# Three stages in one program per engine, with each stage's first steps inside the last steps of the one ahead

## The chip, the cores and the metric

The kernel runs on one core of one Trainium2 chip. The metric is the device time of one execution in microseconds (us), lower is better. The time before is 2320.34 us, the median of three runs (2317.63 to 2322.99).

## The reference

The input is `x`, 16 batches of 512 tokens with 256 features, all float32. Four sublayers follow one another, each with a residual sum and a layer norm:

```python
x = layernorm(x + attention(x))      # 16 heads, causal, rotary; keys and queries go through a latent of 32
x = layernorm(x + fp4_ffn(x))        # gate and up 256 -> 704, silu(gate) * up, down 704 -> 256;
                                     # inputs and weights rounded to FP4 in blocks of 16 along the features
x = layernorm(x + recurrence(x))     # state_t = tanh(state_{t-1} @ tanh(a) + x_t @ b), 16 heads of 64 states,
                                     # out_t = state_t @ c + skip * x_t, then x_t + out_t @ w_out + b_out
x = layernorm(x + channel_mix(x))    # needs the token before each token
```

Attention takes one batch at a time and needs all of its tokens. The feed-forward layer takes any token by itself. The recurrence takes one time step of all 16 batches, and each step needs the one before it.

## The kernel before, in words

`program` calls four functions: `attention`, `fp4_ffn`, `recurrence`, `channel_mix`. Each opens a block of its own (`with nc.Block()`), with one program for each of SyncE (SP, which issues the DMAs), GpSimd (POOL), ScalarE (ACT), VectorE (DVE) and TensorE (PE). At the end of a block all engines wait for one another, and SP waits until the block's last store has landed. Between the functions the activations lie in device memory as rows [512 tokens, 16 batches, 256].

**Attention** is written out in full (`straight`). Step i is one batch and has four cycles g = 0 to 3, one for each group of four heads. The work on a group is spread over several cycles, so after the last group (cycle 63) PE still has the product with the values, the transposes, and the two halves of the output projection to do (L717, L645, L733, L573). Then DVE adds the residual and takes the statistics (L430, L480), POOL makes the scale (L302 to L308), ACT writes the normalised rows (L381) and SP stores them (L247). A batch's rows are stored some six cycles after its last group.

**The feed-forward stage** (`fp4_ffn`) has 64 tiles of 128 rows. A tile is 8 time steps of all 16 batches, so the first tile needs all of attention. `pipelined` writes out the steps -4 to 7, loops over 8 steps at a time, and writes out the last 8 steps and 6 more. In step i PE does gate(i) (L1273), the transposes of hidden tile i-2 (L1297), up(i) (L1273), the transposes of input tile i+1 (L1308), and down(i-2) (L1280). DVE does the residual and statistics of tile i-3, the block scales of input tile i+3, one rounding for input tile i+2 and hidden tile i-1 together (L1240 to L1248), and silu times up for tile i (L1255). POOL multiplies by the scales (L1158 to L1170). PE and DVE hand tiles to one another through counts of semaphores. A table of ACT has to be loaded once for the silu.

**The recurrence** has 64 tiles too, of 8 time steps and 16 batches. In each time step PE multiplies the states of two sides q = 0, 1 by the weights (L1570, L1573) and ACT takes the tanh (L1474) of each side, while PE works on the other. Between the time steps of tile i PE puts the other work: mix (L1619, L1622) and project (L1601) of tile i-1, turn (L1647) and the input products `feed` (L1588, L1591) of tile i+1. Ahead of tile 0 lie a block of set-up (clearing the state on DVE, L1480, and the tanh of the weights on ACT, L1460), the normalisation of tile 0, and 58 matmuls that compute nothing of use (`fill`, L1610). The tiles are then in a loop of two tiles a round:

```python
step(-1, 1)
with pe.Fori(0, 2) as again:
    with pe.Fori(again, 1 + (TILES // 2 - 1) * again) as k:
        for j in range(2):
            step(k * 2 + j, j)
    fill(1, TURN, 32, False)
step(TILES, 0)
```

So tiles 0 and 1 run, then 32 `fill` matmuls, then tiles 2 to 63 by the same code, then 32 `fill` again and what is left of tile 63.

**Channel mix** is a block of its own in both kernels.

Of the kernel before, what the change touches and what calls it, by code (L numbers as in the profile page):

```python
# [6 lines left out]
F32 = mybir.dt.float32  # L7
# [6 lines left out]
P = 128  # L14
# [4 lines left out]
FFN = 704  # L19
# [24 lines left out]

def head_of(g, t):

    return 8 * (g // 2) + 2 * t + g % 2
# [13 lines left out]
class FfnWeights:  # L61

    def __init__(self, nc, ctx):
        def sb(name, shape):
            return ctx.enter_context(nc.sbuf_tensor("kept_" + name, shape, F32))

        self.ident = sb("ident", [P, P])
        self.w_upT = sb("w_upT", [P, CC, 2 * FFN])
        self.w_downT = sb("w_downT", [P, DOWN_CHUNKS, DIM])  # L70
        self.loaded = ctx.enter_context(nc.semaphore("kept_loaded"))

def attention(nc, a, x1_dram, kept):

    with ExitStack() as ctx:
        def sb(name, shape, dt=F32):
            return ctx.enter_context(nc.sbuf_tensor(name, shape, dt))

        def sem(name):  # L80
            return ctx.enter_context(nc.semaphore(name))

        ps_near = ctx.enter_context(nc.psum_tensor("ps_near", [P, GROUP, SEQ], F32))
        near = [ps_near[:, t, :] for t in range(GROUP)]
        far = [ctx.enter_context(nc.psum_tensor(f"ps_far{t}", [P, SEQ], F32))[:] for t in range(GROUP)]

        squares = sb("squares", [P, 2, P])
        ident, blocks = squares[:, 0, :], squares[:, 1, :]
        mask = sb("mask", [P, SEQ])
        ident_bf = sb("ident_bf", [P, P], BF16)  # L90
        ones_bf = sb("ones_bf", [P, P], BF16)
        cos_sin = sb("cos_sin", [P, 2, SEQ])
        cos_t, sin_t = cos_sin[:, 0, :], cos_sin[:, 1, :]
        columns = sb("columns", [P, 10])
        b_attn = columns[:, 0:6]
        q2l_b, kv2l_b, l2o_b, wqk_b = (columns[:, 6 + n:7 + n] for n in range(4))
        probsT = sb("probsT", [P, 2, GROUP, TURNED])
        w_v = probsT[:, 1, GROUP - 1, TURNED - CC * DIM:].rearrange("p (s c) -> p s c", c=DIM)
# [4 lines left out]
        kv2l_rep, l2o_rep = reps[:, 0, :], reps[:, 1, :]  # L103
        bd_v = sb("bd_v", [P, P])
        wc_t = sb("wc_t", [P, CC, DIM])
        cv = sb("cv", [P, CC, DIM])
        by = sb("by", [P, CC])
        by_all = sb("by_all", [P, CC, P])
        bias_row = sb("bias_row", [P, DIM])
        exponent = sb("exponent", [P, QT])  # L110
        eps = sb("eps", [P, QT])

        xT = sb("xT", [P, CC, SEQ])
        xtok = sb("xtok", [P, QT, DIM])
        xb = sb("xb", [P, QT, DIM])
# [6 lines left out]
        k_swap = sb("k_swap", [P, 2, SEQ])  # L122
        Q = sb("Q", [P, GROUPS, SEQ])
        K = sb("K", [P, GROUPS, SEQ])
        V = sb("V", [P, 2, QT, HEADS, LATENT])
# [16 lines left out]

        quantiser = WeightQuantiser(nc, ctx, kept, ident, sem)
# [64 lines left out]

        FIRST_LOADS, LOADS = 16 * 5, 16 * 6

        with nc.Block() as block:
            @block.sync
            def _(sp):
                FIRST = ((w_qk16, a["c_attn_wT"].rearrange("(c p) n -> p c n", p=P)), (columns, a["columns"]), (w_lat, a["w_lat"]),
                         (cos_sin, a["cos_sin"]), (w_qf, a["w_qf"]))
                THEN = ((reps, a["reps"]), (squares, a["squares"]), (w_v, a["c_attn_w_v"].rearrange("(s p) c -> p s c", p=P)),
                        (wc_t, a["cproj_wT"].rearrange("(s p) c -> p s c", p=P)), (bias_row, a["cproj_b"].partition_broadcast(P)),
                        (mask, a["mask"]))
                sp.dma_start(xT[:], a["xT"][0, :, :].rearrange("(c p) t -> p c t", p=P)).then_inc(xT_loaded, 16)
                for dst, src in FIRST:  # L220
                    sp.dma_start(dst[:], src).then_inc(first_loaded, 16)
                for dst, src in THEN:
                    sp.dma_start(dst[:], src).then_inc(loaded, 16)

                def swap(b, g):

                    sp.wait_ge(k_sin_ready, cyc(1, b, g, 3))
                    for i in range(2):
                        sp.dma_start(k_swap[i:P:2, g % 2, :], k_sin[1 - i:P:2, g % 2, :]).then_inc(k_swapped[g % 2], 16)

                def swap_latent(b, g):

                    s = (g + 1) % 2
                    sp.wait_ge(q_turned, cyc(2, b, g, 7))
                    for i in range(2):
                        sp.dma_start(q_swap[i:P:2, s, :], q_sin[1 - i:P:2, s, :]).then_inc(q_swapped[s], 16)

                def step(i, j, k):
                    if isinstance(i, int) and i == -1:
                        sp.dma_start(kept.ident[:], a["ident"]).then_inc(kept.loaded, 16)  # L240
                    for g in range(GROUPS):
                        if g == 1 and exists(i, 0):
                            await_count(sp, xb_ready, i)
                            sp.dma_start(xtok[:], a["x"][bass.ds(i, 1), :, :].rearrange("a (t p) c -> p (a t) c", p=P)).then_inc(xtok_loaded, 16)
                        if g == 2 and exists(i, -2):
                            sp.wait_ge(x1_ready, i - 1)
                            sp.dma_start(x1_dram[:, bass.ds(i - 2, 1), :].rearrange("(t p) a c -> p t (a c)", p=P), x1[:]).then_inc(x1_stored, 16)  # L247
                        if g == 3 and exists(i, 2):
                            sp.wait_ge(V_full, 2 * i + 4)
                            sp.dma_start(xT[:], a["xT"][bass.ds(i + 2, 1), :, :].rearrange("a (c p) t -> p (a c) t", p=P)).then_inc(xT_loaded, 16)  # L250
                        if runs(i, g, 3):
                            swap_latent(i, g)
                        if runs(i, g, 2):
                            swap(i, g)
                        if is_cycle(i, g, 0):
                            quantiser.load(sp, a)
                pipelined(sp, step, BATCH, 2, 1, 2)
                sp.wait_ge(x1_stored, 16 * BATCH)

            @block.gpsimd  # L260
            def _(pool):
                nc.gpsimd.memset(shift[:], 0.0)
                nc.gpsimd.memset(ones_bf[:], 1.0)
                nc.gpsimd.memset(V[:, :, :, :, HEAD_DIM:HEAD_DIM + 1], 1.0)
                nc.gpsimd.memset(V[:, :, :, :, HEAD_DIM + 1:], 0.0)
                nc.gpsimd.memset(eps[:], LN_EPS)
                nc.gpsimd.memset(exponent[:], -0.5)
                nc.gpsimd.memset(zero[:], 0.0).then_inc(constants, 1)
                pool.wait_ge(constants, 1)
                pool.wait_ge(first_loaded, FIRST_LOADS)  # L270

                def add_latent(b, g):

# [6 lines left out]
                def turn_keys(b, g):  # L280
# [5 lines left out]
                    if runs(b, g, 3):  # L286
                        add_latent(b, g)
# [1686 lines left out]
```

## Time and profile before

| what | us |
|---|---|
| median of 3 runs | 2320.34 |
| the profiled execution: its time | 2320.48 |
| its span | 2318.7 |
| attention, by the trace | 0 to 1031.6 |
| feed-forward | 1031.6 to 1577.9 |
| recurrence | 1577.9 to 2114.0 |
| channel mix | 2114.0 to 2318.7 |

How to read it: the stages follow one another without overlap, so the time is their sum. Inside a stage the timeline of an engine gives start, length, line and, in square brackets, the idle time ahead of an instruction and what ended it.
### The profile page before, as it was taken

What the parts mean: (1) busy time and instruction counts of PE and PEld (TensorE: products, weight loads), DVE (VectorE), ACT (ScalarE), POOL (GpSimd) and SP (SyncE); (2) the same over time, 40 slices, a digit from 0 to 9 for tenths busy, and PEclk for the clock granted to TensorE, in tenths of its full rate; (3) what the DMA queues carried; (4) which work ended last, traced back from release to release, by engine and by line L of the source; (5) the groups of instructions that cost most, each with busy time, mean ns of one, the idle gap of its engine ahead of it and who ended that gap; (6) DMA issues with size and microseconds to landing.
All of it is one profiled execution on the core that took longest, in us unless ns stands there. A gap on an engine that the chain in (4) does not pass through costs nothing. (4 is left out here: it accounts for less than half of the span.)

```text
span 2318.7 us, 90879 instructions
## 1 busy us (share of the span) xinstructions
PE 2209.4 (95%) x36556; PEld 1542.3 (67%) x36556; DVE 1706.9 (74%) x4854; ACT 1060.6 (46%) x2707; POOL 1187.8 (51%) x1674
## 2 busy tenths in 40 slices
PE   6999999999999999959999999997999999997997
PEld 3556665556655555536777777776888888885775
DVE  3788888888887777749999999982555555454997
ACT  2656565655666665532222222231444444442444
POOL 3555555655555555525666666662444444441333
PEclk8999999999999999989999999997999999998999
DMA  2211111111111111120100000100101011011232
GB/s 92 91 56 64 57 65 65 65 63 58 57 64 65 65 61 60 52 69 22 33 32 32 32 32 32 34 20 29 32 32 36 32 34 33 32 32 46 84 95 77
DMA packets 101627, 117.73 MB, mean 51 GB/s; under 512 B 10672, under 2 KB 80080, under 8 KB 101456
## 3 DMA queue, kind: packets, MB, share of 16 engines
q1 hardware_dynamic: 101456, 115.44, 15.1%
q8 instruction: 108, 1.77, 0.3%
q14 instruction: 63, 0.52, 0.1%
HBM read 48.29 MB, written 33.55 MB: 35 GB/s over the span
## 5 line engine op out<-in xcount | busy, mean ns | idle before, releaser
L1474 ACT ACTIVATE r_state<-ps_state 128x64 f32<-128x64 f32 x1024 | 228.6, 223 | 295.8 <-PE ps_state L1573 290.7
L1570 PE MATMUL ps_state<-r_state,later_pairs_a 64*64 64x32 f32 x8192 | 334.4, 219 | 19.4 <-ACT r_state L1474 12.5
L1570 PEld LDWEIGHTS ps_state<-r_state,later_pairs_a 64*64 64x64 f32 x8192 | 295.2, 135 | 79.2 <-issue 60.7
L1573 PE MATMUL ps_state<-r_state,later_pairs_a 64*64 64x32 f32 x8192 | 334.6, 220 | 2.8 <-issue 2.8
L423 DVE CUSTOM_DVE_ANT_0 ps_near<-ps_near,mask 128x512 f32<-128x512 f32 (+1 forms) x512 | 270.5, 589 | 89.5 <-PE ps_near L519 89.3
L295 POOL TENSOR_SCALAR_AFFINE_SELECT probsT<-probsT 128x512 f32<-128x512 f32 x256 | 159.8, 636 | 271.2 <-ACT probsT L406 168.0
L1573 PEld LDWEIGHTS ps_state<-r_state,later_pairs_a 64*64 64x64 f32 x8192 | 288.8, 135 | 3.1 <-issue 3.1
L423 DVE CUSTOM_DVE_ANT_0 ps_far<-ps_far,mask 128x384 f32<-128x384 f32 (+1 forms) x512 | 198.3, 457 | 32.7 <-PE ps_far L519 31.7
L1158 POOL TENSOR_TENSOR f_fp<-f_rounded,f_scale 128x960 f32<-128x960 f32 (+2 forms) x67 | 117.3, 1750 | 166.2 <-DVE f_rounded L1248 166.2
L527 PE MATMUL ps_far<-Q,K 32*128 32x256 f32 (+2 forms) x1536 | 180.9, 415 | 1.2 <-ACT probsT L403 0.5
L1181 ACT ACTIVATE f_silu<-ps_gate 128x704 f32<-128x704 f32 x64 | 48.5, 758 | 288.5 <-PE ps_gate L1273 288.5
L1280 PE MATMUL ps_down<-kept_w_downT,f_hT 128*128 128x256 f32 x768 | 176.6, 380 | 1.9 <-ACT f_hT L1186 1.9
L519 PE MATMUL ps_near<-K,Q 32*128 32x512 f32 (+1 forms) x1024 | 165.5, 527 | 9.4 <-POOL K L290 6.3
L406 ACT ACTIVATE probsT<-ps_far 128x512 f32<-128x512 f32 x256 | 132.2, 603 | 89.8 <-PE ps_far L533 89.8
L1273 PE MATMUL ps_gate<-kept_w_upT,f_xT 128*128 128x352 f32 x512 | 164.2, 464 | 1.4 <-ACT f_xT L1195 1.4
L527 PEld LDWEIGHTS ps_far<-Q,K 32*128 32x128 f32 x1536 | 129.1, 183 | 49.9 <-issue 24.9
L1273 PE MATMUL ps_up<-kept_w_upT,f_xT 128*128 128x352 f32 x512 | 162.1, 459 | 0.0
L1452 POOL TENSOR_TENSOR r_veps<-r_mv,r_eps 128x1 f32<-128x1 f32 x64 | 12.2, 190 | 283.8 <-DVE r_mv L1537 283.8
L717 PE MATMUL ps_near<-probsT,V 128*32 128x512 f32 (+3 forms) x2048 | 152.8, 439 | 3.6 <-POOL probsT L295 2.8
L1280 PEld LDWEIGHTS ps_down<-kept_w_downT,f_hT 128*128 128x128 f32 x768 | 141.0, 190 | 19.1 <-ACT f_hT L1186 2.4
L284 POOL TENSOR_TENSOR k_sin<-K,cos_sin 128x512 f32<-128x512 f32 x64 | 81.2, 1269 | 129.1 <-ACT K L367 129.1
L423 DVE DVE_READ_ACCUMULATOR2_ANT top<- 128x1 f32 x1024 | 142.8, 139 | 0.0
(213 smaller groups left out, 5401.1 us busy)
## 6 DMA issues: line engine op xcount, KB each, us to landing
q_swap<-q_sin SPq DMA_DIRECT2D x128, 128.0 KB, 2.1
k_swap<-k_sin SPq DMA_DIRECT2D x128, 128.0 KB, 2.1
xT<-in_xT_dram SPq DMA_DIRECT2D x16, 512.0 KB, 3.6
xtok<-in_x_dram SPq DMA_DIRECT2D x16, 512.0 KB, 3.8
x_rows<-x SPq DMA_DIRECT2D x16, 512.0 KB, 2.9
f_x<-x_rows SPq DMA_DIRECT2D x64, 128.0 KB, 2.0
x_rows<-f_x SPq DMA_DIRECT2D x64, 128.0 KB, 1.7
r_x<-x_rows SPq DMA_DIRECT2D x64, 128.0 KB, 2.1
```

The lines of the kernel that those rows point to most:

```text
L295: return nc.gpsimd.affine_select(block, block, pattern=[[0, GROUP], [1, P]], compare_op=ALU.is_ge, fill=0.0, base=0, channel_multiplier=-1)
L406: nc.scalar.activation(mine[:, t, AT[1]:AT[1] + SEQ], far[t], ACT.Exp).then_inc(exped, 1)
L423: nc.vector.tensor_tensor_reduce(bank[:, at:at + width], bank[:, at:at + width], mask[:, SEQ - width:SEQ], 1.0, -3e38, ALU.add, ALU.max, t ...
L519: out = nc.tensor.matmul(bank[:, at:at + width], Q[rows, g, qi * P:(qi + 1) * P], K[rows, g, 0:width], start=True, stop=True, skip_group_c ...
L527: return nc.tensor.matmul(bank[:, at:at + SEQ - kj * P], K[rows, g, kj * P:(kj + 1) * P], Q[rows, g, kj * P:SEQ], start=(kj != 3), stop=Fa ...
L717: out = nc.tensor.matmul(near[0][LATENT * t:LATENT * (t + 1), kj * P:SEQ], V[:, jp, kj, head_of(gp, t), :], probsT[:, gp % 2, t, AT[kj]:AT ...
L1158: nc.gpsimd.tensor_tensor(blocks(parts(fp4[:, s, :], i, BLOCK)), blocks(parts(rounded[:, s, :], i, BLOCK)), spread(parts(scale[:, s, :], i ...
L1273: out = nc.tensor.matmul(ps[:, half, 0:HALF], xT[:, j % 2, c, :], w_upT[:, c, at + half * HALF:at + (half + 1) * HALF], start=(c == 0), st ...
L1280: out = nc.tensor.matmul(ps_down[:, 0:DIM], hT[:, j % 2, kd, :], w_downT[:, kd, :], start=(kd == 0), stop=(kd == KD - 1))
L1474: nc.scalar.activation(state[:, j % 2, banks, :, t, 0, :], sums[:, j % 2, banks, :, now], ACT.Tanh).then_inc(state_ready[t], 1)
L1570: nc.tensor.matmul(sums[half(v), j % 2, stays, c, now], A[half(v), 3 * q, c, :], last[half(v), stays, c, :], start=False, stop=True, skip_ ...
L1573: out = nc.tensor.matmul(sums[half(1 - v), j % 2, changes, c, now], A[half(v), 3 * q + 1 + was, c, :], last[half(v), changes, c, :], start ...
```

## The change

Attention, the feed-forward stage and the recurrence now share one block. Each of them returns its five engine programs (`Programs`) in place of running them, and for the feed-forward stage each is an object `Steps`, whose `to(n)` issues the steps up to n. The attention programs call `feed.to` inside their last cycles, and the recurrence programs call it ahead of and inside their first tile.

```diff
+class Steps:
+    def to(self, end):
+        unroll = self.unroll
+        while self.at < end:
+            if self.at == unroll and end >= self.tiles - unroll > unroll:
+                with self.engine.Fori(1, self.tiles // unroll - 1) as k:
+                    for j in range(unroll):
+                        self.step(k * unroll + j, j, k)
+                self.at = self.tiles - unroll
+            else:
+                self.step(self.at, self.at % unroll, self.at // unroll)
+                self.at += 1
```

Where attention calls it (cycle 63 is the last group, 64 to 67 the four after it; here and for the recurrence below, the added lines are put together by engine):

```diff
 # SP
+if is_cycle(i, g, CYCLES - 2):
+    sp.wait_ge(quantiser.copied, len(quantiser.fills))
+    feed.to(4)
 # POOL, around the first affine select of the last group, and after cycle 65
+if is_cycle(i, g, CYCLES - 1): feed.to(-2)
+if is_cycle(i, g, CYCLES - 1): feed.to(0)
+if is_cycle(i, g, CYCLES + 1): feed.to(3)
 # ACT: after yT of cycle 63; after its last Exp; after cycle 65
+if is_cycle(i, g, CYCLES - 1): feed.to(0)
+if is_cycle(i, g, CYCLES - 1): feed.to(1)
+if is_cycle(i, g, CYCLES + 1): feed.to(3)
 # DVE: after y of cycle 63; then behind the attention work of cycles 64, 65 and 67
+if is_cycle(i, g, CYCLES - 1): feed.to(0)
+if is_cycle(i, g, CYCLES): feed.to(1)
+elif is_cycle(i, g, CYCLES + 1): feed.to(2)
+elif is_cycle(i, g, CYCLES + 3): feed.to(3)
 # PE: ahead of the product with the values of the last group; and behind cycles 63, 65 and 67
+if is_cycle(i, g, CYCLES):
+    pe.wait_ge(exped, 12 * CYCLES - 2)
+    feed.to(1)
...
+if is_cycle(i, g, CYCLES - 1):
+    pe.wait_ge(exped, cyc(12, i, g, 4))
+    feed.to(0)
+elif is_cycle(i, g, CYCLES + 1):
+    feed.to(2)
+elif is_cycle(i, g, CYCLES + 3):
+    pe.wait_ge(z_added, 2 * BATCH)
+    feed.to(3)
```

A feed-forward tile is now 128 tokens of one batch, in rows 16 KB apart; tile n of the first 16 waits only for batch n's store, and the loads of the recurrence's weights move from step 0 to step 12 (`LATER`). SP's part is written out for all 64 tiles:

```diff
+def rows(dram, n):
+    return dram[n // BATCH * P:(n // BATCH + 1) * P, n % BATCH, :]
...
+if n < BATCH:
+    sp.wait_ge(x1_stored, 16 * (n + 1))
+sp.dma_start(x[:, n % UNROLL, :], rows(x1_dram, n)).then_inc(x_loaded[n % UNROLL], 16)
```

The second half of the last output projection goes to another PSUM bank (`near[2]`), so it no longer waits for DVE to empty the first. The PSUM banks of the stages and the SBUF tiles are laid out so that the first steps use what the stage ahead has left.

At the recurrence (FED is 64, LAST_FED is 2; feed-forward step 64 is the hidden transposes and down of tile 62, step 65 those of tile 63):

```diff
 # SP
+feed.to(FED - 8); wait for the first 16 stores; steps.to(1); feed.finish(); steps.finish()
 # POOL: the clearing of the state between feed-forward steps 4 to 7
+feed.to(FED - 2); steps.to(-1); feed.to(FED - 1); steps.to(0); feed.finish(); steps.finish()
 # ACT
+feed.to(FED); nc.scalar.activation(A[:], A[:], ACT.Tanh); feed.to(FED + 1)
+# and feed.to(FED + 2) at time step LAST_FED of tile 0
 # DVE
+measure(-2, 2, -1); feed.to(FED - 1); normalise(-2, 2); measure(-1, 3, -1)
+feed.to(FED); normalise(-1, 3); turned(-1, 3); feed.finish(); steps.finish()
 # PE
+feed.to(FED)
+pe.wait_ge(xn_ready, 1); turn(-1, 1, MIX[1])
+feed.to(FED + 1)
+pe.wait_ge(xT_ready, 1); pe.wait_ge(*fed[0])
+for c in range(CC): out = inputs(-1, c)
...
+step(0, 0)                       # with feed.finish() ahead of time step LAST_FED
+with pe.Fori(0, 2) as again:
+    with pe.Fori(again, 1 + (TILES // 2 - 2) * again) as k:
+        for j in (1, 2):
+            step(k * 2 + j, j % 2)
+    fill(0, TURN, 32, False)
+step(TILES - 1, 1)
 step(TILES, 0)
```

Tile 0 and tile 63 are now written out ahead of and behind PE's loop, with tiles 1 and 2 in its first round. The 58 `fill` matmuls ahead of tile 0 are gone; those behind the first round and behind the loop stay, the latter now ahead of tile 63. Tile 0 leaves out mix and project, tile 63 leaves out turn and `feed`. `feed(j, c)` of before is called `inputs(j, c)`.

## Rows read from the trace of the kernel before

**Rows 1.** The profile page: each engine's busy time, its share and instructions.
```profile
PE 2209.4 (95%) x36556; PEld 1542.3 (67%) x36556; DVE 1706.9 (74%) x4854; ACT 1060.6 (46%) x2707; POOL 1187.8 (51%) x1674
```
**Rows 2.** Windows: start:end, length, busy time of each engine, PEclk, DMA.
```profile
1003.00:1031.60 28.60, 12.43 (x136) 6.78 (x136) 7.51 (x24) 7.64 (x17) 7.16 (x12) 0.84 0.11 37
1031.60:1061.89 30.29, 21.55 (x75) 13.94 (x76) 24.28 (x57) 5.89 (x10) 9.56 (x14) 0.81 0.31 98
1061.89:1553.99 492.10, 492.10 (x2162) 366.00 (x2161) 464.20 (x957) 142.07 (x299) 332.21 (x420) 1.00 0.10 31
...
1588.18:1601.20 13.02, 9.80 (x358) 8.17 (x360) 1.39 (x5) 3.57 (x16) 3.98 (x9) 0.80 0.08 23
1601.20:1614.50 13.30, 12.61 (x346) 10.78 (x341) 3.96 (x12) 3.57 (x16) 1.93 (x7) 0.50 0.01 4
1614.50:1620.70 6.20, 6.20 (x44) 4.35 (x33) 0.00 (x0) 0.00 (x0) 1.38 (x2) 0.57 0.15 45
1620.70:1628.40 7.70, 7.47 (x348) 6.31 (x346) 3.68 (x12) 3.57 (x16) 0.90 (x3) 1.00 0.00 0
```
**Rows 3.** Timeline of PE at the end of attention: start, us, line, count, idle.
```profile
1008.73 4.06 PE L717 MATMUL ps_near<-probsT,V 128*32 128x512 f32 x32 [2.81 <-POOL probsT L295]
...
1017.06 1.93 PE L573 MATMUL ps_near<-wc_t,yfT 128*32 128x256 f32 x32 [1.01 <-DVE yfT L490]
...
1019.91 1.93 PE L573 MATMUL ps_near<-wc_t,yfT 128*32 128x256 f32 x32 [0.91 <-DVE z L430]
...
1037.94 0.66 PE L1308 MATMUL ps_xT<-kept_ident,f_fp 128*128 128x128 f32 x2 [16.10 <-POOL f_fp L1158]
```
**Rows 4.** Timeline of DVE and of ACT behind the last projection.
```profile
1021.91 0.69 DVE L430 TENSOR_TENSOR z<-ps_near,xb 128x512 f32<-128x512 f32 x1 [2.06 <-PE ps_near L573]
...
1022.64 1.41 DVE L480 BATCH_NORM_STATS2 stats<-z 128x6 f32<-128x256 f32 x4
...
1026.20 2.07 ACT L381 ACTIVATE x<-z,centre,rstd 128x256 f32<-128x256 f32 x4 [10.79 <-POOL centre L308]
```
**Rows 5.** Timeline of PE: the parts of step 3 of the feed-forward stage.
```profile
1061.89 2.53 PE L1273 MATMUL ps_gate<-kept_w_upT,f_xT 128*128 128x352 f32 x8
1064.25 0.82 PE L1297 MATMUL ps_hT<-kept_ident,f_fp 128*128 128x128 f32 x6
1064.91 2.53 PE L1273 MATMUL ps_up<-kept_w_upT,f_xT 128*128 128x352 f32 x8
...
1067.50 2.75 PE L1280 MATMUL ps_down<-kept_w_downT,f_hT 128*128 128x256 f32 x12
```
**Rows 6.** DMA issues of the page: attention's stores, KB each, us to landing.
```profile
x_rows<-x SPq DMA_DIRECT2D x16, 512.0 KB, 2.9
```
**Rows 7.** Timeline of PE: from the last feed-forward tiles to the recurrence.
```profile
1561.97 0.82 PE L1297 MATMUL ps_hT<-kept_ident,f_fp 128*128 128x128 f32 x6
...
1563.72 2.86 PE L1280 MATMUL ps_down<-kept_w_downT,f_hT 128*128 128x256 f32 x12 [0.94 <-ACT f_hT L1186]
...
1578.85 6.21 PE L1610 MATMUL ps_state<-r_quiet 128*128 128x256 bf16 x40 [6.09 <-ACT later_pairs_a L1460]
...
1595.48 0.30 PE L1573 MATMUL ps_state<-r_state,later_pairs_a 64*64 64x32 f32 x3 [2.13 <-issue]
...
1600.49 0.49 PE L1588 MATMUL ps_state<-r_xT,later_pairs_b 32*64 32x64 f32 x7 [0.94 <-issue]
```
**Rows 8.** DMA traffic within 1593 to 1594 us: the instruction queue, one fetch.
```profile
q8 instruction: 1, 0.02, 5.7%
```
**Rows 9.** Timeline of DVE: the same instruction of tiles 3 and 5.
```profile
1632.35 0.61 DVE L1517 TENSOR_SCALAR r_xT<-ps_state,later_recurrence_columns 128x128 f32<-128x128 f32 x2 [1.46 <-PE ps_state L1647]
...
1647.91 0.61 DVE L1517 TENSOR_SCALAR r_xT<-ps_state,later_recurrence_columns 128x128 f32<-128x128 f32 x2 [1.46 <-PE ps_state L1647]
```
**Rows 10.** Timeline of PE in and behind the recurrence's last tile.
```profile
2101.81 0.29 PE L1591 MATMUL ps_state<-r_xT,later_pairs_b 32*64 32x128 f32 x1 [0.52 <-DVEq L1542]
...
2103.23 3.67 PE L1610 MATMUL ps_state<-r_quiet 128*128 128x256 bf16 x32
```

More of the change, by code:

```diff
@@ L1 @@
+from collections import namedtuple
 from contextlib import ExitStack
@@ L819, in attention_arrays @@
+            straight(step)
+        return Programs(sync, gpsimd, scalar, vector, tensor), early, x1_stored, (exped, 12 * CYCLES)
 def attention_arrays(inputs):
@@ L1323, with recurrence @@
 STEPS = P // BATCH
-def recurrence(nc, ident, weights, x2_dram, x3_dram):
+def recurrence(nc, sems, memory, banks, ident, weights, x2_dram, x2_stored, fed, x3_dram):
     TILES = TOKENS // P
@@ new lines, in recurrence, with exists, later, half @@
+    x3_stored = [sem(f"x3_stored{s}") for s in range(2)]
+    def exists(i, d):
+        return not isinstance(i, int) or 0 <= i + d < TILES
+    def later(i, d, n):
+        return not isinstance(i, int) or i + d >= n
+    def half(v):
+        return slice(v * STATE, (v + 1) * STATE)
+    def steps_of(t, parity):
+        return t.rearrange("p (n e b) -> p n e b", e=2, b=BATCH)[:, :, parity, :]
+    LEAD, LAG = 3, 4
+    FED = TILES
+    LAST_FED = 2
+    def sync(sp, feed):
+        def step(i, j, k):
+            if exists(i, 3):
+                if later(i, 3, UNROLL):
+                    sp.wait_ge(twice_ready, i + (4 - UNROLL))
+                sp.dma_start(x[:, (j + 3) % UNROLL, :], x2_dram[bass.ds((i + 3) * P, P), :]).then_inc(x_loaded[(j + 3) % UNROLL], 16)
+            if exists(i, -3):
+                sp.wait_ge(x3_ready, i - 2)
+                sp.dma_start(x3_dram[bass.ds((i - 3) * P, P), :], x3[:, (j + 1) % 2, :]).then_inc(x3_stored[(j + 1) % 2], 16)
+        steps = Steps(sp, step, TILES, UNROLL, LEAD, LAG)
+        feed.to(FED - 8)
+        for stored in x2_stored:
+            sp.wait_ge(stored, 16 * (BATCH // 2))
+        steps.to(1)
+        feed.finish()
+        steps.finish()
+        for stored in x3_stored:
+            sp.wait_ge(stored, 16 * (TILES // 2))
@@ new lines, in scalar, with step @@
+    def scalar(act, feed):
+        feed.to(FED)
+        act.wait_ge(weights.loaded, 16 * weights.LOADS)
+        nc.scalar.activation(A[:], A[:], ACT.Tanh).then_inc(w_tanh, 1)
+        feed.to(FED + 1)
+        def step(i, j, k):
+            for t in range(STEPS):
+                if isinstance(i, int) and i == 0 and t == LAST_FED:
+                    feed.to(FED + 2)
+                if exists(i, 0):
+                    for q in range(SIDES):
+                        if t == 0:
+                            act.wait_ge(inputs_in, i + 1)
+                        act.wait_ge(summed[q], i * STEPS + (t + 1))
+                        if t == 0 and later(i, 0, 2):
+                            act.wait_ge(mix_full, 2 * i)
+                        now, banks = slice(t * BATCH, (t + 1) * BATCH), slice(2 * q, 2 * q + 2)
+                        nc.scalar.activation(state[:, j % 2, banks, :, t, 0, :], sums[j % 2][:, banks, :, now], ACT.Tanh).then_inc(state_ready[t], 1)
+        steps = Steps(act, step, TILES, UNROLL, LEAD, LAG)
+        steps.to(1)
+        feed.finish()
+        steps.finish()
```

2151 lines of the change are left out of this document (1094 added, 1057 removed).

## The prediction

> **What bounds the kernel now.** I read the page's busy times first. PE is busy for 2209.4 of 2318.7 us [rows 1], so a change that removes no PE work can win only in the gaps, or where PE is busy but slow. The view of windows then says where these are [rows 2]. From 1061.89 to 1553.99 PE is busy all the time: 60 feed-forward tiles, 492.10 / 60 = 8.20 us each. Its order there is gate, transposes, up, transposes, down [rows 5]. DVE is busy for 464.20 / 60 = 7.74 us a tile, close behind. From tile 3 on the recurrence repeats every (1647.91 - 1632.35) / 2 = 7.78 us a tile [rows 9]. Neither rate is touched. Three stretches are bad. (a) From 1003 to 1061.89 PE has 12.43 + 21.55 us of work in 58.9 us [rows 2]: the tail of attention, a barrier, and a pipeline that fills. PE idles 16.10 us in one piece ahead of the first feed-forward transposes [rows 3]. (b) From 1561.97, the hidden transposes of tile 62, to the first recurrence matmul at 1588.18: 26.2 us with two tiles' down in it. (c) From 1588.18 to 1628.40 the recurrence does three tiles in 40.2 us where 3 x 7.78 = 23.3 would do. The reader should see PEclk fall to 0.50 there and stay for all of tile 1 [rows 2].
>
> The sum is made against the profiled execution: 2320.48 us, of which the span is 2318.7. The median of the runs, 2320.34, is the same to 0.14 us. All times below are on the clock of the trace of before.
>
> **Change (a), attention to feed-forward.** I replay the order written in the diff until PE starts the gate of tile 3, which was at 1061.89 and from which PE never waits. A step of feed-forward on PE has the parts gate 2.36, hidden transposes 0.66, up with input transposes 2.59, down 2.6 (starts apart) [rows 5].
> - Steps -4 to -1 need DVE and POOL, which have little to do in cycle 63. I cost them at nothing, covered by PE's and ACT's work on the last group, but for 0.9 us on PE and ACT (two transposes, a copy, and the scores that wait behind them). If that cover is not there, PE waits for up to 6 us, from DVE's work in the stretch that begins at 1031.60 (24.28 us, of which some 6 lie ahead of the first gate) [rows 2].
> - Step 0 on PE (gate, up, transposes: 5.0 us) goes ahead of the product with the values. PE idled there from 1008.73 - 2.81 = 1005.92 [rows 3]; with the 0.9 it starts at 1006.8 and ends at 1011.8. The product took 4.06 us [rows 3] with PEclk at 0.50 after that idle time; with PE kept busy I take 2.4, down to 1014.2 against 1012.8. So step 0 costs the tail 1.4 us.
> - Copy, transposes, division and transposes again (4.3 us before, 1012.8 to the next projection at 1017.06) shift by 1.4, and step 1, for which the projection now waits, begins at 1017.9 at the latest. It ends at 1022.9. The two halves of the projection, 1.93 each [rows 3], end at 1026.8.
> - DVE is in program order too: it begins step 1 at about 1019, has 7.7 us of it, then adds the two halves, 0.69 each [rows 4]: 1028.1. PE waits for this count before step 2.
> - Step 2 on PE, 8.2 us: gate of tile 3 at 1036.4.
> - Behind DVE's step 2 come the last batch's statistics and POOL's scale (1026.20 - 1022.64 = 3.6 us up to ACT's start) and ACT's write (2.07) [rows 4]: 1028.1 + 0.7 + 7.8 + 3.6 + 2.1 = 1042.3, ahead of ACT's silu and copy of step 3. PE wants that copy for down at 1043.5 and gets it at 1044.9: 1.4 us.
> Gain: 1061.89 - 1036.4 - 1.4 = 24.1 us. Bounds: at most 27 (no stall in step 3, and the product hides step 0); at least 12, if step 3 as a whole waits behind the last batch's rows.
>
> The order of tiles costs nothing that I can find. The loads run four tiles, 33 us, ahead; the trace does not show 1 KB rows at 16 KB distance for 128 KB, but attention's stores of four times as much have that distance and land in 2.9 us [rows 6]. Even 10 us a load would be hidden. SP's loads of tiles 8 and later stand behind the last batch's store, at about 1044, and tile 8 is wanted after 1054.
>
> **Change (b), feed-forward to recurrence.** PE's step 63 ends at 1561.97. Then, in order: the turn of tile 0 (0.4), hidden transposes of tile 62 (0.8), ACT's copy (0.94 idle) [rows 7], down (2.8): 1566.9. DVE's part for tile 0, some 3 us over steps 61 to 63, lies in its slack of 8.20 - 7.74 us a tile and in the shorter last steps. The input products take 0.9 us: time step 0 begins at 1567.8, not at 1588.18. The 58 `fill` (6.21 us for 40 of them) [rows 7], the set-up and the barrier fall away. After two time steps (1.9) tile 63's transposes, copy and down come in, 0.8 + 0.9 + 2.7 = 4.4 us in which the recurrence stands still: 1574.1. Six more time steps at 0.97: tile 0 ends at 1580. At full clock without stalls the old tile 0 would have ended at 1588.18 + 7.78 = 1595.96. This part is worth 16 us. The bound below is 11: DVE a whole 5 us late with tile 0's input.
>
> **(c) The slow start of the recurrence.** In tile 0 PE stands for 2.13 us with nothing to wait for ("issue"), and 0.94 us again at its end [rows 7]. A fetch on the instruction queue falls in the first gap [rows 8]: this is code that runs for the first time, at 348 / 7.70 = 45 matmul records a microsecond when nothing stops it [rows 2]. Then the clock is 0.50; tile 1 takes 13.30 us, and the 32 `fill` take 6.20 us and bring 1.00 back [rows 2]. In the new order all of tile 0 is first-time code, and so are tiles 1 and 2, the loop's first round. The 4.4 us of slow work inside tile 0 let the fetching catch up, so I put the same stall of 2.1 at the end of tile 0 and the fall right behind it. Then tiles 1 and 2 are both at half clock: 1580 + 2.1 + 2 x 13.3 + 6.2 = 1614.9 for the start of tile 3, against 1628.4. So of the 16 us here 13.5 are left. This is the term with ends far apart. If the clock never falls, it is 1580 + 15.6 + 3.7 = 1599.3, a gain of 29; if the stall comes in tile 0's third time step, five steps more at half clock cost 3 and the gain is 10.
>
> **The end.** Tile 63 leaves out turn, `feed` and a wait of 0.52 [rows 10]: 0.4 + 0.9 + 0.5 = 1.8 saved. The `fill` of 3.67 only changes place. But tile 63 is now first-time code: I add the stall of 2.1 and 2.0 for three time steps at half clock, which is what tile 0 paid from 1595.5 to 1601.2 (5.7 against 3.7). Net +2.3, bounds -1.8 and +4.
>
> Here the Trainium skill speaks otherwise ("Runtime: NRT & Kernel Launch", section "Instruction fetch mechanics"): the prefetch is sequential, straight code is mostly hidden by the issue rate, and it is taken branches that stall. By that rule the first run of a straight tile would cost nothing. The row with 2.13 us of "issue" in code that is reached without a backward branch disagrees, so I go by the row; what the rule would make of the time is the first rival.
>
> Two small edits go together: the clearing of the state moves to POOL between early feed-forward steps, under 1 us a piece. POOL is busy for 332.21 of 492.10 us [rows 2] and idles before each of its multiplications, so it is hidden; if not, it costs 2 us once.
>
> **Sum.** -24.1 - 13.5 + 2.3 = -35.3: 2320.48 - 35.3 = 2285 us.
>
> **Rivals.**
> 1. *The clock stays up.* For it: PE comes out of dense work, and the down of tile 63 lies inside tile 0. The rule of the Trainium skill named above ("Runtime: NRT & Kernel Launch", "Instruction fetch mechanics"), that straight code is fetched in time, would have this result. Against it: PE starved at this code rate once [rows 2, 7]. Then -24.1 - 29 - 1.8 = -55: 2265 us.
> 2. *The steps of the two stages get into each other's way at (a).* In-order engines: ACT's write of the last batch or DVE's two sums hold up the filling pipeline. For it: three engines carry both, and DVE has 7.7 us of work a step ahead of each small piece of the tail. Against it: the positions in the replay fit. Then (a) gives 12 to 14: 2295 to 2297 us.
> 3. *Slower: the clock is not regained.* The `fill` after the first round is what brought 1.00 back. If a fall comes behind it, say when PE jumps back to the loop's start, nothing in the recurrence restores it, since tile 1 alone at 13.30 us a tile did not. Each tile then costs 13.3 - 7.8 = 5.5 us, and it decides from the seventh tile (35 / 5.5); over 61 tiles 2285 + 336 = 2621 us. Against it: the same `fill` before the same backward jump held it for 62 tiles.
> 4. *It does less than it says:* a wait that I have not seen serialises one of the seams, (a) or (b), and the time is 2300 to 2318, or no change.
>
> **How the numbers follow.** Forecast 0.55, rival 1 0.14, rival 2 0.18, rival 3 0.04, rival 4 0.09, of which 0.03 is within 0.2% (5 us, about what a measurement of this kernel can tell from no change) and 0.01 slower. The forecast's own range is 2276 to 2291, from the ends of (c) and of the tail. The range 2264 to 2300 takes in rivals 1 and 2 and leaves out 0.13. Faster 0.92, same 0.03, slower 0.05.
>
> **What would show it.** In the changed trace: the gate of tile 3 near 1036 to 1040, PE without a gap over 3 us between 1003 and 1040, and no half clock at the product with the values (a); from the hidden transposes of tile 62 to the first L1570 matmul 6 us, where it was 26.2 (b); a gap named "issue" of about 2 us near the end of tile 0, PEclk 0.50 over the two tiles behind it and 1.00 after the `fill` (c); a second such gap in tile 63. Wrong would be: DVE's sum of the last projection more than 3 us behind it, the gate of tile 3 after 1045, PEclk at 1.00 all the way, or 0.50 behind the first round.

## The result, and the profile after

The changed kernel takes 2283.43 us (median of 4, 2282.18 to 2286.24); the kernel before took 2320.43 beside it (2317.63 to 2322.99). The ratio is 0.984, with a 95% interval of 0.9825 to 0.986. The forecast was 2285, so the sum came out. Its terms did less well: the one for the end of the recurrence was off by 4.1 us, those for (a) and (c) by 1.6 and 1.4 us in the opposite direction, so the closeness of the sum is in part luck. One of the 35 executions of the kernel before, which stands in no ratio here and has no trace, took 3662.56 us at a mean granted clock of 0.543.

The profiled execution took 2283.54 us with a span of 2281.8, which is 36.9 less than the span of before. The page's line for the engines, which answers to [rows 1]:

```profile
PE 2199.1 (96%) x36408; PEld 1534.9 (67%) x36408; DVE 1706.3 (75%) x4852; ACT 1060.1 (46%) x2707; POOL 1191.2 (52%) x1676
```

PE has only 10.3 us less work, so 26.6 of the 36.9 came out of its gaps. The view of windows, as in [rows 2] (start:end, length, busy time of each engine with its instructions, PEclk, DMA share, GB/s), shows the stretches that answer to those of before:

```profile
994.00:996.00 2.00, 0.59 (x4) 0.51 (x8) 1.86 (x8) 1.36 (x3) 1.05 (x2) 0.86 0.00 0
996.00:1002.00 6.00, 5.19 (x32) 1.29 (x28) 3.24 (x12) 2.06 (x4) 2.55 (x5) 0.50 0.00 0
1003.00:1037.92 34.92, 31.55 (x255) 20.41 (x244) 26.75 (x60) 12.10 (x24) 15.93 (x18) 1.00 0.05 16
1047.56:1531.46 483.90, 483.90 (x2126) 359.96 (x2125) 456.89 (x940) 140.22 (x295) 327.89 (x423) 1.00 0.12 36
1545.30:1557.00 11.70, 10.23 (x340) 8.44 (x341) 3.64 (x11) 5.36 (x21) 5.38 (x17) 1.00 0.05 15
1557.00:1562.00 5.00, 3.16 (x138) 2.61 (x133) 0.69 (x2) 1.68 (x8) 2.16 (x4) 1.00 0.19 56
1562.00:1587.00 25.00, 21.17 (x543) 17.29 (x535) 7.23 (x22) 5.56 (x25) 6.62 (x16) 0.50 0.08 24
1587.00:1593.30 6.30, 6.30 (x61) 4.62 (x58) 0.00 (x0) 0.24 (x2) 0.00 (x0) 0.54 0.14 43
1593.30:1601.50 8.20, 8.00 (x359) 6.65 (x357) 3.57 (x11) 3.57 (x16) 0.74 (x2) 1.00 0.00 0
2063.30:2071.00 7.70, 6.93 (x321) 5.93 (x320) 2.54 (x8) 3.57 (x16) 0.74 (x2) 1.00 0.02 5
```

The reader should see five things. The tail of attention now has PE busy for 31.55 of 34.92 us at full clock. The steady feed-forward tile is what it was: 483.90 / 59 = 8.20 us from the gate of tile 4 to that of tile 63. The recurrence's tile 0 runs at full clock (1545.30 to 1557.00). The clock then stands at 0.50 from 1562 until the `fill` brings it back, up to 1593.3. And tile 63 (the last line) is at 1.00 from end to end.

The seam between attention and feed-forward, timeline of PE, answering to [rows 3 to 5]:

```profile
995.41 2.09 PE L580 MATMUL ps_near<-Q,K 32*128 32x512 f32 x8 [1.67 <-ACT shiftT L401]
998.73 4.09 PE L773 MATMUL ps_near<-probsT,V 128*32 128x512 f32 x32 [0.81 <-ACT probsT L415]
...
1009.43 2.63 PE L1342 MATMUL ps_gate<-kept_w_upT,f_xT 128*128 128x352 f32 x8 [0.54 <-ACT probsT L448]
1011.90 2.53 PE L1342 MATMUL ps_up<-kept_w_upT,f_xT 128*128 128x352 f32 x8
...
1014.58 2.36 PE L773 MATMUL ps_near<-probsT,V 128*32 128x512 f32 x32
...
1029.61 2.63 PE L1342 MATMUL ps_gate<-kept_w_upT,f_xT 128*128 128x352 f32 x8 [0.86 <-DVE z L475]
...
1037.92 2.53 PE L1342 MATMUL ps_gate<-kept_w_upT,f_xT 128*128 128x352 f32 x8
...
1044.86 2.86 PE L1349 MATMUL ps_down<-kept_w_downT,f_hT 128*128 128x256 f32 x12 [1.18 <-ACT f_hT L1259]
1047.56 2.53 PE L1342 MATMUL ps_gate<-kept_w_upT,f_xT 128*128 128x352 f32 x8
```

Gate 0 stands ahead of the last product with the values, which takes 2.36 us where it took 4.06; gate 3 is at 1037.92. The last gap before the steady tiles is the 1.18 us for ACT's copy in step 3.

The seam between feed-forward and recurrence, answering to [rows 7]: PE, and then ACT's tanh, of which there is one per time step.

```profile
1539.65 0.82 PE L1368 MATMUL ps_hT<-kept_ident,f_fp 128*128 128x128 f32 x6
1541.41 2.86 PE L1349 MATMUL ps_down<-kept_w_downT,f_hT 128*128 128x256 f32 x12 [0.94 <-ACT f_hT L1259]
...
1548.51 2.86 PE L1349 MATMUL ps_down<-kept_w_downT,f_hT 128*128 128x256 f32 x12 [0.94 <-ACT f_hT L1259]
1561.03 0.24 PE L1687 MATMUL ps_state<-r_state,later_pairs_a 64*64 64x32 f32 x1 [1.78 <-issue]
```
```profile
1545.82 0.46 ACT L1575 ACTIVATE r_state<-ps_state 128x64 f32<-128x64 f32 x2 [3.96 <-PE ps_state L1690]
1546.60 0.46 ACT L1575 ACTIVATE r_state<-ps_state 128x64 f32<-128x64 f32 x2 [0.32 <-PE ps_state L1690]
1551.80 0.46 ACT L1575 ACTIVATE r_state<-ps_state 128x64 f32<-128x64 f32 x2 [2.84 <-PE ps_state L1690]
...
1558.37 0.46 ACT L1575 ACTIVATE r_state<-ps_state 128x64 f32<-128x64 f32 x2 [0.58 <-PE ps_state L1690]
1561.38 0.48 ACT L1575 ACTIVATE r_state<-ps_state 128x64 f32<-128x64 f32 x2 [2.56 <-PE ps_state L1690]
```

From the hidden transposes of tile 62 to the first recurrence matmul it is 5.6 us, where it was 26.2. The jump from 1546.60 to 1551.80 is tile 63's down inside tile 0 (a normal step is 0.8 to 1.0, so 4.4 are added). The jump to 1561.38 is the first stall: two time steps of tile 1 are done, and PE stands still in the third for "issue". Three more such gaps follow, the last of them longer than the first:

```profile
1566.79 0.21 PE L1687 MATMUL ps_state<-r_state,later_pairs_a 64*64 64x32 f32 x1 [0.97 <-issue]
...
1571.78 0.32 PE L1687 MATMUL ps_state<-r_state,later_pairs_a 64*64 64x32 f32 x2 [0.98 <-issue]
...
1584.66 0.21 PE L1687 MATMUL ps_state<-r_state,later_pairs_a 64*64 64x32 f32 x1 [1.88 <-issue]
```

Where the 36.9 us came from, in differences between the same two events of each trace:

| stretch | before | after | gain |
|---|---|---|---|
| attention's start to the gate of tile 63 | 1553.99 | 1531.46 | 22.5 |
| gate of tile 63 to the first tanh | 34.7 | 14.4 | 20.4 |
| first tanh to tile 3's first tanh | 40.2 | 48.5 | -8.3 |
| tile 3's first tanh to channel mix | 485.1 | 483.3 | 1.8 |
| channel mix | 204.6 | 204.1 | 0.5 |

### The profile page after: what moved, and what is told of

Read it like the earlier page. It is cut to its first block and busy times, and to the rows that moved or that the text cites. A ratio compares the mean times of both kernels' runs of the same rounds, so it can differ in the third digit from the quotient of the medians.

```text
span 2281.8 us, 90273 instructions
## 1 busy us (share of the span) xinstructions
PE 2199.1 (96%) x36408; PEld 1534.9 (67%) x36408; DVE 1706.3 (75%) x4852; ACT 1060.1 (46%) x2707; POOL 1191.2 (52%) x1676
```

## The experiments

Each was timed beside the kernel before on its chip. "Start" below is the time from the gate of tile 63 to tile 3's first tanh in the run's trace: 62.9 us in the changed kernel, 75.0 before. It leaves out what moves ahead of the seam.

**e1: no feed-forward steps inside attention.**

```diff
-if is_cycle(i, g, CYCLES - 1): feed.to(...)     # all calls of POOL, ACT, DVE and PE in attention
-...
 if is_cycle(i, g, CYCLES + 3):
     pe.wait_ge(z_added, 2 * BATCH)
-    feed.to(3)
```

> The changed kernel without the feed-forward steps inside attention: GpSimd, ScalarE, VectorE and TensorE begin step -4 only when their own attention work is done; one block, per-batch tiles and early loads stay. Theory (the steps inside the tail hide the filling of the pipeline; the barrier is the smaller part): VectorE can start filling at about 1024.5 us instead of 1033.6, so the gate of tile 3 comes near 1053 (1061.9 before, 1037.9 changed); time about 2298 us, 14 to 16 above the changed kernel. Rival (dropping the barrier and the store-and-load round trip is what pays, the interleaving adds little): 2284 to 2287 us.

2298.61 us (2298.43 to 2303.34), ratio 0.991 (0.989 to 0.993). PE's timeline shows what is left of the seam:

```profile
1011.92 2.36 PE L750 MATMUL ps_near<-probsT,V 128*32 128x512 f32 x32 [2.81 <-POOL probsT L330]
...
1029.55 0.66 PE L1353 MATMUL ps_xT<-kept_ident,f_fp 128*128 128x128 f32 x2 [7.33 <-POOL f_fp L1203]
1030.67 4.28 PE L1313 MATMUL ps_gate<-kept_w_upT,f_xT 128*128 128x352 f32 x8 [0.46 <-ACT f_xT L1239]
```

So the steps inside attention are worth 15 of the 22.5 us. The other 7 come from what this kernel still has: one block in place of three, the early loads and the order of the tiles.

**e2: e1, and the tiles in the old order.** SP's early loads go too, since the first of them now waits for the last store.

```diff
 # SP, in attention
-feed.to(4)
...
-return dram[n // BATCH * P:(n // BATCH + 1) * P, n % BATCH, :]
+return dram.rearrange("t b c -> (t b) c")[n * P:(n + 1) * P, :]
...
-if n < BATCH:
-    sp.wait_ge(x1_stored, 16 * (n + 1))
+if n == 0:
+    sp.wait_ge(x1_stored, 16 * BATCH)
```

> As the kernel without steps inside attention, and the feed-forward tiles are again 128 consecutive rows (8 time steps of all batches), so the first load waits for the last batch's store. Theory (tiles of one batch cost nothing in the steady state and are worth only the wait for the last store): first load at about 1031 us, gate of tile 3 near 1061, time about 2305 us, 7 to 9 above the kernel without heads; steady feed-forward tile 8.20 us in both. Rival (rows 16 KB apart slow the stage): steady tile below 8.20 us here, and the time at or under that of the kernel without heads.

2309.73 us (2306.71 to 2312.83), ratio 0.9955 (0.994 to 0.997), 11.1 more than e1. The first gate is at 1040.18 against 1030.67: 9.5 of it.

```profile
1039.06 0.66 PE L1352 MATMUL ps_xT<-kept_ident,f_fp 128*128 128x128 f32 x2 [15.65 <-POOL f_fp L1202]
1040.18 5.06 PE L1312 MATMUL ps_gate<-kept_w_upT,f_xT 128*128 128x352 f32 x8 [0.46 <-ACT f_xT L1238]
```

The wait is the 16.10 of [rows 3] again. A tile of one batch pays by itself, before any step is moved, because it needs one batch's store only. One block without the barrier brings next to nothing at this seam: from DVE's last sum of attention (1023.48 here, 1021.91 before) to the gate of tile 3 it is 40.1 us, where it was 40.0. Nor do rows 16 KB apart cost anything: from the gate of tile 4 to that of tile 63 both e1 and e2 take 485.6 us.

**e3: tile 63's down ahead of tile 0.** The pause of 4.4 us is put in front of the first-time code.

```diff
-    LAST_FED = 2
+    LAST_FED = 0
```

> The last feed-forward tile is finished ahead of time step 0 of the recurrence instead of ahead of time step 2. Theory A (a pause in the dense code lets the instruction fetch catch up, and the next stall comes some 8 us of dense work after it): the stall that is in time step 2 of tile 1 comes two time steps earlier, at the border of tiles 0 and 1, and the half clock with it; tile 3 starts 1 to 3 us later against the gate of tile 63, about 0.8 of it because TensorE waits for the last transposes' input; time about 2285.5 us. Theory B (the stall sits at a fixed place in the code): the stall stays in time step 2 of tile 1; only the 0.8 us is lost, 2284.2 us.

2287.69 us (2286.79 to 2290.26), ratio 0.985 (0.984 to 0.987); start 66.2, 3.3 more. The stall (1.51 us of "issue") is again in the third time step of tile 1, as B had it, but the time is 3.5 us over B's. 1.0 of that is a new wait of the hidden transposes for POOL. Another 1.7 is what it brings about: the clock is at 0.50 from 1551.3 to 1554.7 us, and tile 63's down takes 4.54 us in place of 2.86.

**e4: tile 63's down later in tile 0.**

```diff
-    LAST_FED = 2
+    LAST_FED = 5
```

> The last feed-forward tile is finished ahead of time step 5 instead of 2. Theory A (pause lets the fetch catch up): the stall moves three time steps later, to about time step 5 of tile 1, fewer time steps run at half clock: tile 3 starts about 2 us earlier against the gate of tile 63, 2281.4 us. Theory B (fixed place in the code): the stall stays in time step 2 of tile 1 and the time within 0.5 us of the changed kernel's 2283.4.

2283.28 us (2279.25 to 2284.25), ratio 0.983 (0.981 to 0.985); start 60.8. The third time step of tile 1 has no gap now; the first one ends at 1569.29 (2.50 us of "issue"), in the sixth time step.

**e5: a pause of 12 `fill` behind tile 0.**

```diff
         step(0, 0)
+        fill(0, TURN, 12, False)
         with pe.Fori(0, 2) as again:
```

> Edit: 12 more fill matmuls (0.117 us each at full clock, 1.4 us) between recurrence tile 0 and the loop. Theory (the first-time code is fetched more slowly than PE runs through it, and any 1.4 us in which PE needs no new code pushes the stall later): the stall of 1.9 us, now after time step 1 of tile 1, comes some six time steps later or more, so six or more time steps run at full clock instead of half (0.6 to 0.7 us each): +1.4 - 4 to 5 = about 2280 us against 2283.4. Rival (the stall belongs to a fixed place of the code): stall after time step 1 of tile 1 again, +1.4, 2284.8 us.

2281.16 us (2279.32 to 2282.82), ratio 0.983 (0.981 to 0.985); start 60.6, with its 1.4 us in it. The longest gap (2.22 us) is in the sixth time step of tile 1. The rival's fixed place is not gone: a gap of 1.10 us still stands in the third time step, but the clock stays at 1.00 behind it until 1569.5. Three time steps were won, not six.

**e6: a short `fill` ahead of tile 63.** This asks for the term that the prediction had wrong: why tile 63, first-time code too, had no stall.

```diff
-            fill(0, TURN, 32, False)
+            with pe.Fori(0, 4 - 3 * again):
+                fill(0, TURN, 8, False)
```

> Edit: of the 32 fill matmuls ahead of the recurrence's last tile only 8 are left (0.9 us instead of 3.7); those behind the loop's first round stay at 32. Theory A (tile 63, first-time code, ran without a stall because the fill gives the fetch 3.7 us in which PE needs no new code): a stall of some 2 us inside tile 63 and half clock behind it, so the 2.8 us saved are given back: 2283 to 2285 us. Rival B (tile 63 needs no such pause): no stall, the 2.8 us are a gain, 2280.6 us.

2281.48 us (2281.01 to 2283.54), ratio 0.983 (0.982 to 0.985). The median looks like B and the trace like A. From tile 3's first tanh to channel mix it is 482.9 us against 483.3, so of 2.6 us less `fill` 0.4 are left. PE's timeline and the windows at the end of this kernel's recurrence:

```profile
2058.09 1.05 PE L1727 MATMUL ps_state<-r_quiet 128*128 128x256 bf16 x8
...
2066.41 0.23 PE L1690 MATMUL ps_state<-r_state,later_pairs_a 64*64 64x16 f32 x2 [0.65 <-issue]
...
2068.38 1.98 PE L1718 MATMUL ps_state<-later_w_outT,r_outs 64*64 64x256 f32 x16 [0.21 <-DVE r_outs L1636]
```
```profile
2066.00:2068.00 2.00, 1.17 (x52) 1.07 (x52) 0.44 (x2) 0.45 (x2) 0.64 (x2) 0.99 0.00 0
2068.00:2070.00 2.00, 1.79 (x23) 0.80 (x16) 0.58 (x2) 0.00 (x0) 0.00 (x0) 0.50 0.22 74
```

With the pause cut short a stall appears, and half clock behind the last time step. From the first tanh of tile 63 to its last it is 1.26 us more, and from there to channel mix 0.89. The median's 2 us came from the start (61.2), whose code was not edited. There the gap in the third time step of tile 1 was only 0.96 us, and the long one, 2.78 us, stood in the sixth.

**e7: the recurrence's start not interleaved.** Every engine finishes feed-forward first; no barrier and no `fill` come back.

```diff
 # POOL, ACT, DVE and PE, ahead of their part of the recurrence
-feed.to(FED - 2); feed.to(FED)
+feed.finish()
```

> Edit: at the recurrence's start every engine first finishes the feed-forward stage and then begins its part of the recurrence (no barrier, attention's seam unchanged). Theory (the steps of the two stages lying inside each other are worth 12 to 13 us here, of which the barrier and the 58 fill matmuls are a part): 2292 to 2298 us. Rival (the gain came from the fill matmuls and the barrier alone, interleaving is worth nothing): within 3 us of 2283.4.

2294.45 us (2293.86 to 2295.82), ratio 0.989 (0.987 to 0.990), 11.0 above the changed kernel; start 73.5. PE stands idle for 4.12 and 2.50 us for DVE's part, the clock falls ahead of the first time step, and tile 0 is at 0.50 as well.

**e8: a short `fill` behind the first round.** This tries the slower rival's price.

```diff
-            fill(0, TURN, 32, False)
+            with pe.Fori(0, 1 + 3 * again):
+                fill(0, TURN, 8, False)
```

> Edit: of the 32 fill matmuls behind the loop's first round (tiles 1 and 2) only 8 are left; those ahead of tile 63 stay at 32. Theory (the recurrence's own matmuls do not bring the clock back; it is the fill that does): tiles 3 to 62 stay at half clock, 60 x (13.3 - 7.8) = +330 us less 4.5 for the missing fill, about 2609 us. Rival (the recurrence brings its clock back by itself, or 8 fills do): 2279 to 2300 us.

Four executions: 2282.23, 2576.01, 2280.55 and 2573.01 us. The mean granted clock was 0.982 in the first and 0.837 in the second. Neither theory had both. The first is the one with a trace (start 57.9 us, the missing `fill` less).

**e9: one `fill` behind the first round.**

```diff
-            fill(0, TURN, 32, False)
+            with pe.Fori(0, 1 + 31 * again):
+                fill(0, TURN, 1, False)
```

> Edit: behind the loop's first round 1 fill matmul is left of 32; the 32 ahead of tile 63 stay, each with one jump of a loop. With 8 left, two of four executions took 2281 us and two 2575. Theory (the clock stands at half after tile 2 in every execution, the recurrence's own work does not raise it, and dense matmuls behind the first round do; 8 of them reach that point in some executions only): with 1 left every execution is slow, 2574 to 2580 us, PEclk 0.50 from tile 1 to the fill ahead of tile 63. Rival (which executions are slow is chance of another kind, not the length of the fill): fast and slow executions again.

2584.62 us (2583.11 to 2585.39), ratio 1.113 (1.110 to 1.115): all four executions took this long. One window over 37 tiles, and DVE's same instruction in two of them:

```profile
1590.00:2063.00 473.00, 472.72 (x12932) 396.28 (x12928) 149.93 (x448) 133.67 (x599) 122.17 (x296) 0.50 0.06 21
```
```profile
1593.80 0.61 DVE L1609 TENSOR_SCALAR r_xT<-ps_state,later_recurrence_columns 128x128 f32<-128x128 f32 x2 [2.92 <-PE ps_state L1747]
1606.42 0.61 DVE L1609 TENSOR_SCALAR r_xT<-ps_state,later_recurrence_columns 128x128 f32<-128x128 f32 x2 [2.92 <-PE ps_state L1747]
```

PE is busy for 99.9% of 473 us and the clock stays at 0.50. A tile takes 12.62 us instead of 7.78. The recurrence does not bring its clock back by itself; the `fill` does.

**e10: both pauses.** The edits of e4 and e5 in one kernel.

```diff
-    LAST_FED = 2
+    LAST_FED = 5
...
         step(0, 0)
+        fill(0, TURN, 12, False)
```

> Edit: LAST_FED = 5 in place of 2, and 12 fill matmuls between tile 0 and the loop (both fills of 32 stay). Theory (each pause in which PE needs no new code puts off the stall and with it the half clock): the two add up, LAST_FED 5 being worth about 2 us by the trace of the start (tile 3 at 60.8 instead of 62.9 us behind the gate of tile 63) and the fill ahead 2.3 by the medians: 2279 us, tile 1 at full clock throughout. Rival (one pause is enough, a second only costs its own length): 2281 to 2285.

2281.01 us (2280.15 to 2282.45), ratio 0.982 (0.980 to 0.984); start 60.6. The longest gap (2.50 us) ends at 1566.01, in the sixth time step of tile 1, where it is with either pause alone. The two don't add up; the theory of pauses that add is wrong here.

**e11: the changed kernel again**, with no edit, and **e12: e10 and the short `fill` of e6**, timed side by side.

> The changed kernel itself, once more, for two questions that one profile left open. Theory (where the stall in the recurrence's first-time code comes, and whether the clock falls at the last output projection but one, vary from execution to execution of the same code): another time step for the stall, between the tenth and the fifteenth of the recurrence, and the gate of feed-forward tile 63 anywhere within 3 us; median 2283.4 again. Rival (both are fixed by the code, and what e3 to e10 moved they moved by their edits): stall in front of the third time step of tile 1 and PEclk 0.50 at 996 to 1002 us again.

> Edit: LAST_FED = 5, 12 fill matmuls between tile 0 and the loop, and 8 of the 32 ahead of tile 63 left; the one to beat is the changed kernel of the same call. Theory (each is worth what its own run gave: the pauses 2.4 us together, the short last fill 0.5 by its trace): 2280.5 us, 2.9 under the changed kernel. Rival (the differences of 2 us between these medians are chance of the call): within 1 us of the changed kernel.

e11 took 2284.41 us (2280.13 to 2287.38), e12 2280.29 (2277.67 to 2284.20); ratios 0.983 (0.981 to 0.985) and 0.9815 (0.980 to 0.983). e12 is 4.1 us under e11, though the two ranges overlap. The traces give 3.3 of it to the start (60.1 against 63.4) and nothing to the short `fill` (483.7 in both behind it; e12 has gaps of 0.55 and 1.02 us in tile 63, e11 none). e11's first stall was in tile 1's third time step again, its gate of tile 63 at 1534.64 where it had been 1531.46. e12 has the lowest median: 3 to 4 us below the changed kernel's own (2283.4 and 2284.4), and 0.7 below e10's.

## Why the prediction was right, and where it was not

**(a) 24.1 us predicted, 22.5 measured.** The replay held at every step that it named: gate 0 ahead of the product, 2.36 us for the product, 0.86 of waiting for DVE's two sums (predicted 1.3), step 3's stall 1.18 (predicted 1.4). One reason in it is not borne out: that the product takes 2.4 us because PE is kept busy. In e1 and e2 PE idles ahead of it for 2.81 us as before, and it takes 2.36 us too, at a clock of 1.00. e1 and e2 show the two halves: 15.2 us for the moved steps (median of e1 against the changed kernel's) and 10.4 for the tile order (gate of tile 63 at 1546.98 in e1, 1557.37 in e2), less the 3.4 by which e2 is behind the 1553.99 of before (1.6 of that it had lost in attention already, and 1.7 in feed-forward tiles 6 to 9, as e1 did). The replay began from the time of before at 1003 us, and there it lost 2.6 us. At 995 to 1002 the clock was 0.50 behind an idle time of 1.67 us, so scores took 2.09 and the product with the values 4.09 us. In the trace of before, the same idle time at the same place left it at 1.00:

```profile
995.69 1.14 PE L527 MATMUL ps_near<-Q,K 32*128 32x512 f32 x8 [1.67 <-ACT shiftT L361]
997.87 2.36 PE L717 MATMUL ps_near<-probsT,V 128*32 128x512 f32 x32 [0.82 <-ACT probsT L375]
```

It is not the moved steps that do it: e1 has none, and its product took 4.50 us. The windows of e1 to e12 all show 0.50 within 996 to 1004. The trace of before had its half clock one cycle earlier, and for 3.4 us in place of 6.8:

```profile
981.60:985.00 3.40, 3.40 (x19) 2.01 (x21) 0.42 (x1) 0.71 (x2) 0.00 (x0) 0.51 0.00 0
```

What decides between the two was not settled; before has only the one trace.

**(b) 20.4 predicted, 20.4 measured, and the freeze of 4.4 as well.** That "such a seam is a barrier and 58 `fill`" would be the wrong reading. e7 has neither and loses 11.0 us, since PE idles for DVE and the clock falls at once.

**(c) 13.5 predicted, 12.1 measured.** The mechanism held: PE stalls for "issue" in first-time code, and the clock is at half behind it until the `fill`. The prediction had one stall of 2.1 us, at the end of tile 0. The trace has the first two time steps later, in tile 1 (1.78 us), and three more behind it (0.97, 0.98 and 1.88 us), of which the sum had only the 0.68 us that lies in its 13.30 for a tile. The later start wins two time steps at full clock, some 1.3 us, and the further gaps take it back and more. The Trainium skill's rule ("Runtime: NRT & Kernel Launch", "Instruction fetch mechanics"), that straight code is mostly hidden by the issue rate, would have had no stall. The trace of the changed kernel and those of e1 to e12 all have one, the longest gap in each between 1.5 and 2.8 us. The row of the prediction was the better guide.

**The end: +2.3 predicted, -1.8 measured.** This step failed: "tile 63 is now first-time code: I add the stall of 2.1 and 2.0 for three time steps at half clock". Tile 63 is first-time code, but it stands behind 3.7 us of `fill`, in which PE runs 32 matmuls. The prediction said that slow work lets the fetching catch up, used that for tile 0, and did not use it here. e6 shows it: with 8 `fill` a stall comes (0.65 us in one piece), and half clock behind the last time step. e12, with the same 8, has gaps of 0.55 and 1.02 us there. In e6 tile 63 and what follows it up to channel mix cost 2.2 us more, not the 4.1 that was put down; 8 `fill` are a pause too, and without any the case wasn't tried.

The two errors of 1.6 and 1.4 on the gains and this one of 4.1 nearly cancel. With channel mix's unforeseen 0.5 that is 36.9 for 35.3. The 0.5 is not shown to be an effect of the change: the stage takes 203.6 to 204.8 us in the traces of e1 to e12, where its code is the same. That the sum came out is luck to this extent.

**The slower rival** was priced at 5.5 us a tile, from a tile that had stalls of its own in it. e9 measured 12.62 - 7.78 = 4.84, and 301 us in all, where 336 was said. Its mechanism is real and was nearer than a chance of 0.04 sounds: with 8 in place of 32 `fill`, two of four executions took as long as e9's, at the same mean clock (0.837 and 0.838; e9 0.833). They have no trace.

**Where the gaps stand.** The traces answer a question that e3 to e6 and e10 left. The gaps stand at fixed borders in PE's code, some 245 matmuls and weight loads apart. The windows between the ends of one gap and the start of the next show it, for the changed kernel (first two lines) and for e6 (last two); the first counts in brackets are PE's matmuls, the second its weight loads:

```profile
1561.03:1566.78 5.75, 4.79 (x122) 3.78 (x123) 2.18 (x7) 1.56 (x7) 0.00 (x0) 0.59 0.17 48
1566.79:1571.77 4.98, 4.00 (x125) 3.53 (x125) 1.08 (x4) 1.11 (x5) 3.31 (x8) 0.50 0.02 5
...
1560.49:1566.44 5.95, 3.19 (x122) 2.58 (x123) 3.27 (x10) 1.57 (x7) 1.16 (x4) 0.98 0.15 47
1566.45:1571.43 4.98, 4.01 (x125) 3.53 (x125) 0.00 (x0) 1.12 (x5) 2.16 (x4) 0.50 0.17 56
```

The changed kernel, e6, e8, e9 and e11 have their gaps in the same places: the third and the sixth time step of tile 1, the start of tile 2, and its seventh time step. e9 has one of 0.45 us at the start of tile 1 besides. Only the lengths differ. In the third and the sixth they are 1.78 and 0.97 us (changed kernel, e9), 0.96 and 2.78 (e6), 1.51 and 1.51 (e8, e11). The 12 `fill` of e5 and e10 shift the border in the sixth time step by a dozen matmuls. Each gap ends shortly behind a fetch on the instruction queue, as the one of [rows 8] does. The changed kernel's DMA traffic within 1564.5 to 1566 us, ahead of the gap that ends at 1566.79:

```profile
q8 instruction: 1, 0.02, 3.9%
```

The 14 traces have 54 such gaps of 0.45 us or more in the recurrence, and each ends 1.1 to 1.8 us behind the landing of a fetch. Between tiles 4 and 62, where PE's loop repeats, no trace has a fetch on that queue, and none has such a gap. So the stall is a wait for instructions. Both theories of e3 and e4 had a part: the places are fixed, and in e4, e10 and e12, with the pause late in tile 0, the gap in the third time step is gone.

**Open.** What shares the waiting out among the borders in executions of the same code. With a pause late in tile 0 or behind it (e4, e5, e10, e12) the first gap of over 1.5 us stood in the sixth time step, and the start took 60.1 to 60.8 us, against 61.2 to 63.4 in the changed kernel, e1, e2, e6 and e11. A gap of 0.96 to 1.23 us in the third time step (e6, e5, e2) left the clock at 1.00 until the longer one in the sixth, and those of 1.51 and 1.78 us there had 0.50 within 2 us behind them.

## What to carry to other kernels

Before joining two stages, replay the first steps engine by engine in program order. If the first unit of the next stage can be cut so that it needs only an early part of the last stage's output, that alone may pay (10 us here). Price every stretch of dense code that runs for the first time with a stall at several of its fetch borders (four in two tiles here, 5.6 us together) and the half clock behind the first long one. A few microseconds of sparse code directly ahead hid all of it for a stretch of 8 us, but not for one of three tiles. If a loop of small matmuls can't raise its own clock, look how the clock is raised ahead of it and how near that is to failing: here 32 dense matmuls did it in all 47 executions of the changed kernel and the variants that kept them, 8 in two of four, 1 in none of four.

## What the runs showed of the hardware

In e9 PE was busy for 99.9% of 473 us, at 27 matmul records a microsecond, and stayed at the lower of its two levels (1.2 GHz) all that time. With 8 `fill` ahead of it the same code ran either way, 2281 or 2575 us, and nothing in between. Granted clock and stalls also differ from one execution to the next in untouched code: the gate of tile 63 stood between 1530.0 and 1535.0 us in the traces of kernels that are alike up to there. A part of this is one more stretch of 3.4 us at 0.50 near 360 us: e3, e4, e7, e8, e11 and e12 have it, and their gate stands at 1533.1 or later; the others don't, and theirs stands at 1532.0 or earlier. So a difference of 2 us between two medians says little here, until the trace shows in which stretch it lies.
